# First attention: PSUM banks regrouped from three and three to four and two

## What is computed

```python
q = (hidden_states @ Wq.T).reshape(B, S, H, D)      # S = 1024, H = 32 heads, D = 8
k, v = ...                                          # likewise; rope on q and k
scores = jnp.einsum('bhid,bhjd->bhij', q, k) * scale
bias = jnp.where(in_band, learnable_bias[:, clip(diag)], 0.0)   # 0 <= i - j < 128
scores = jnp.where(causal, scores + bias, -jnp.inf)
m = jnp.maximum(jnp.max(scores, axis=-1), off)      # a row's maximum
p = jnp.exp(scores - m[..., None])
denom = jnp.sum(p, axis=-1) + jnp.exp(off - m)
out = jnp.einsum('bhij,bhjd->bhid', p, v) / denom[..., None]
```

## Time and profile before

| | us |
|---|---|
| median of 3 runs | 1211.83 (1206.76 to 1213.01) |
| the profiled execution | 1214.93 |
| its span, first to last instruction | 1212.6 |
| first look alone (opening stretch) | 165 to 191.5 |
| eight groups of second look | 191.6 to 493 |

### The profile page before, as it was taken

The page is one execution under the profiler, slowest core; times in us unless marked ns, Lnnn a source line. Parts: engine busy times, 40 slices in busy tenths (PEclk is TensorE's granted clock), DMA queues, the critical chain, the costliest instruction groups (busy, mean ns, idle before and its releaser), DMA issues.

```text
span 1212.6 us, 21037 instructions
## 1 busy us (share of the span) xinstructions
PE 1015.3 (84%) x7768; PEld 671.0 (55%) x7768; DVE 812.0 (67%) x1979; ACT 584.5 (48%) x1231; POOL 319.0 (26%) x212
## 2 busy tenths in 40 slices
PE   1798768999999998699787678898988988889697
PEld 1587612333333333478565556676666766667575
DVE  6745887787777771479778546666666666666654
ACT  1533224556656567254444235545445555454264
POOL 4010230000000000000033105555545464555344
PEclk9999857999999999899989699999999999999998
DMA  7010254312332100110121000000000000000001
GB/s 165 1 70 3 87 132 66 60 36 47 62 67 52 27 11 1 36 53 18 70 70 35 1 1 1 2 1 1 2 1 1 1 2 1 2 1 1 1 1 35
DMA packets 24038, 37.12 MB, mean 31 GB/s; under 512 B 2992, under 2 KB 21040, under 8 KB 22160
## 3 DMA queue, kind: packets, MB, share of 16 engines
q1 hardware_dynamic: 23936, 35.78, 12.8%
HBM read 31.31 MB, written 4.27 MB: 29 GB/s over the span
## 4 chain that ended last, share of the span: by engine, by line
PE 62%; DVE 22%; issue 8%; ACT 5%; DMA 1%; SPq 1%; POOL 1%; DVEq 0%; POOLq 0%; ACTq 0%
PE bank L923 18%; PE pair L1207 6%; PE bank L1251 6%; PE bank L1057 6%; PE bank L1086 5%; PE bank L1047 4%; PE bank L989 4%; DVE mx L1586 4%; PE bank L1239 3%; PE bank L1072 3%; ACT PT L825 2%; DVE PT L1619 2%; PE bank L953 2%; DVE bank L1462 2%; DVE hL L1386 1%
## 5 line engine op out<-in xcount | busy, mean ns | idle before, releaser
L705 POOL TENSOR_SCALAR P<-P,rec 128x1024 f32<-128x1024 f32 (+7 forms) x128 | 220.4, 1724 | 228.3 <-DVE rec L1611 228.3
L825 ACT ACTIVATE PT<-bank 128x512 f32<-128x512 f32 (+3 forms) x384 | 165.7, 493 | 103.7 <-PE bank L1072 87.7
L1462 DVE CUSTOM_DVE_ANT_0 bank<-bank,stripS 128x512 f32<-128x512 f32 (+3 forms) x256 | 148.9, 606 | 54.6 <-PE bank L1047 51.7
L1047 PE MATMUL bank<-KT,QT 96*128 96x512 bf16 (+3 forms) x384 | 126.5, 365 | 26.8 <-DVE MX L1462 11.9
L1239 PE MATMUL bank<-ident,P 128*128 128x128 f32 x576 | 99.0, 281 | 45.9 <-DVE PT L1619 33.7
L1057 PE MATMUL bank<-QT,KT 128*128 128x512 bf16 (+3 forms) x384 | 112.9, 336 | 12.9 <-ACT PT L825 11.0
L1207 PE MATMUL pair<-KH,QH 128*128 128x512 f16 (+3 forms) x576 | 115.4, 328 | 5.6 <-ACT P L872 4.2
L1251 PE MATMUL bank<-PT,VH 128*128 128x128 f16 x1728 | 117.2, 219 | 0.1
L872 ACT ACTIVATE P<-pair,nm 128x1024 f32<-128x1024 f32 (+7 forms) x128 | 95.6, 747 | 43.8 <-DVE nm L1590 43.8
L1251 PEld LDWEIGHTS bank<-PT,VH 128*128 128x128 f16 x1728 | 107.1, 98 | 2.8 <-DVE PT L1619 0.2
L1619 DVE TENSOR_TENSOR PT<-bank,PT 128x384 f16<-128x384 f32 (+1 forms) x192 | 99.7, 547 | 11.8 <-ACT PT L713 11.8
(11 more groups left out here) (178 smaller groups left out, 1920.0 us busy)
## 6 DMA issues: line engine op xcount, KB each, us to landing
stripS<-band_rows SPq DMA_DIRECT2D x32, 128.0 KB, 2.1
KT<-qk_dram SPq DMA_DIRECT2D x21, 192.0 KB
qk_dram<-parts SPq DMA_DIRECT2D x12, 256.0 KB, 2.4
cprow<-cp SPq DMA_DIRECT2D x9, 256.0 KB, 11.1
stripT<-seq_dram SPq DMA_DIRECT2D x24, 88.0 KB, 9.1
q_raw<-w_gu SPq DMA_DIRECT2D x4, 512.0 KB, 4.0
w_raw<-w_q SPq DMA_DIRECT2D x2, 1024.0 KB, 5.9
w_raw<-w_dense SPq DMA_DIRECT2D x2, 1024.0 KB, 5.4
```

The lines of the kernel that those rows point to most:

```text
L705: pool.tensor_scalar(rows, rows, rec1[:, m % 4:m % 4 + 1], None, ALU.mult).then_inc(s["pn"], 1)
L825: act.activation(PT[:, jb % 2, h, o:o + ni], bank[2 + i2 % 3][:, 0:ni], ACT.Exp).then_inc(s["s2_exp"], 1)
L1047: pe.matmul(ring_bank(use)[:, 0:nj], queries(g)[0:ROWS, h, P * ib:P * (ib + 1)], KT3[0:ROWS, g % 3, h, j0:j0 + nj], start=True, stop=True) ...
L1462: dve.tensor_tensor_reduce(out, out, stripS[:, h, HALF - nj:HALF], 1.0, LOWEST, ALU.add, ALU.max, mx).then_inc(s["s1_max"], 1)
```

## The change

Bank 5 moves from the ring to the second look. The ring has banks 0 and 1, and a use waits for the use two places earlier; second-look tiles rotate through banks 2 to 5, and product i waits for the exponential of tile i-4. No instruction is added, removed or moved on any engine; the banks of the tiles and the counts of the waits are what differs.

```diff
--- before.py
+++ after.py
@@ -409,14 +409,14 @@
                 RING += [("s", i, 0) for i in look1_at(g, st)] + ([turn(g, st)] if turn(g, st) else [])
         RING += [("o", NG - 1, 0), ("o", NG - 1, 1)]
         at_ring = {u: i for i, u in enumerate(RING)}
-        RING_BANKS = (0, 1, 5)
+        RING_BANKS = (0, 1)
 
         def ring_bank(use):
-            return bank[RING_BANKS[at_ring[use] % 3]]
+            return bank[RING_BANKS[at_ring[use] % 2]]
 
         def wait_ring(eng, use):
 
-            i = at_ring[use] - 3
+            i = at_ring[use] - 2
             if i >= 0:
                 kind, n, h = RING[i]
                 if kind == "s":
@@ -822,7 +822,7 @@
                                 if TB * g + jb >= 2:
                                     act.wait_ge(s["pv"], TB * g + jb - 1)
                                 o = i0 - jb * P
-                                act.activation(PT[:, jb % 2, h, o:o + ni], bank[2 + i2 % 3][:, 0:ni], ACT.Exp).then_inc(s["s2_exp"], 1)
+                                act.activation(PT[:, jb % 2, h, o:o + ni], bank[2 + i2 % 4][:, 0:ni], ACT.Exp).then_inc(s["s2_exp"], 1)
                         if st == 0 and g:
                             outputs(g - 1)
                         use = turn(g, st)
@@ -1052,9 +1052,9 @@
                 i2 = at_s2(g, jb, h, c)
                 if jb == 0 and h % 2 == 0 and c == 0:
                     pe.wait_ge(m_in[h // 2], 32 * (g + 1))
-                if i2 >= 3:
-                    pe.wait_ge(s["s2_exp"], i2 - 2)
-                ins = pe.matmul(bank[2 + i2 % 3][:, 0:ni], KT3[:, g % 3, h, P * jb:P * (jb + 1)], queries(g)[:, h, i0:i0 + ni],
+                if i2 >= 4:
+                    pe.wait_ge(s["s2_exp"], i2 - 3)
+                ins = pe.matmul(bank[2 + i2 % 4][:, 0:ni], KT3[:, g % 3, h, P * jb:P * (jb + 1)], queries(g)[:, h, i0:i0 + ni],
                                 start=True, stop=True)
                 if band_of(i0, ni, jb)[0] <= 0:
                     ins.then_inc(s["s2"], 1)
@@ -1069,7 +1069,7 @@
                     for q in range(4):
                         rows = slice(STRIP_ROWS * q, STRIP_ROWS * (q + 1))
                         first = STRIP_ROWS * (3 - q) + at
-                        ins = pe.matmul(bank[2 + at_s2(g, jb, h, c) % 3][rows, 0:n], flipb[:, :], stripT[:, g % 2, h, first:first + n],
+                        ins = pe.matmul(bank[2 + at_s2(g, jb, h, c) % 4][rows, 0:n], flipb[:, :], stripT[:, g % 2, h, first:first + n],
                                         start=False, stop=True, skip_group_check=True)
                     ins.then_inc(s["s2"], 1)
```

## The result

The changed kernel takes **1253.92 us** (median of 4 runs, 1252.86 to 1256.22) against 1212.42 us for the kernel before in the same comparison (4 runs, 1206.76 to 1216.19). The ratio is **1.0349**, 95% interval 1.0305 to 1.0392: slower by 41.5 us. Forecast were 1250 us and slower, with a range of 1224 to 1268.

What follows compares the result with a forecast made beforehand. DVE bounds the opening; in the groups PE, DVE and ACT form one chain, PE leading. Terms sum to +38.2 us on the profiled 1214.93, giving 1253.1; less 3.1 to the median, 1250 us, range 1224 to 1268.

Steps and rivals of the forecast that it cites:

- opening: First attention, 165 to 191.5 us, 60 first-look tiles, no second look: two banks hold back strip reduces, +9.6 us.
- part 2: Four second-look banks: product i waits for the exponential of i-4 instead of i-3; -1.5 us a group, -1.8 in the last.
- first group: First group of four heads after the opening, without output turns: 6.2 - 1.2 - 1.5 = +3.5 us.
- five usual groups: The five groups of four heads after the first: 6.2 - 1.5 = 4.7 us each, +23.5 us.
- group with 36 tiles: Seventh group, only 36 first-look tiles left: the stalls of steps 0 to 12 and slightly more gain, +3.4 us.
- Part 1: First-look ring from three banks to two: tile i waits for the reduce of i-2; +6.2 us a usual group, opening +9.6.
- the list of second-look waits: Usual group, PE's later waits for ACT: 0.31 (0.30 goes), 0.36, 0.48, 0.17 and 0.17 us; gain summed to -1.5 a group.
- steps 8 to 12: Usual group, where three first-look tiles meet only two of the second look: 2.3 us of the two-bank ring's loss.
- A: Rival: two banks are enough, DVE catches up, only removed ACT waits count after the opening; about -15 us, 1196; chance 0.08.
- B: Rival: stalls and gains cancel in the groups, only the opening and last group count, +9.6 and -1.8, 1220 us; chance 0.10.
- C: Rival: four second-look banks give nothing, as values products pin PE to ACT or it gets no lead; +50.5, 1262; chance 0.12.
- D: Rival: the clock swings, two falls in each of eight groups, 38 + 16 us and more, 1266 and up; chance 0.10.

Runs made afterwards that it cites:

- the kernel without part 2: Against the kernel before, the first look's ring cut from three banks to two, the second look keeping three, bank 5 idle: 1260.24 us, ratio 1.0362.
- forward schedule: Changed banks (two and four) with four first-look tiles in steps 0 to 3, three in 4 to 9, two or three after: 1231.37 us, 1.0143 against the kernel before.
- the even: Changed kernel with three first-look tiles in every step, instead of two in steps 0 and 1 and four in 14 and 15: 1236.45 us, 1.0191 against the kernel before.

## Why the prediction was right, point by point

The sign and the mechanism came out: the ring of two makes PE wait for DVE, in the opening and in every group, and the kernel without part 2 and the one with the opening's third bank back show it. The total is nearer than the terms deserve. The forecast left the clock out of its sum, and said so. The third column below is an estimate of what the banks did: steps that ran at the lower clock in one of the two kernels are replaced by the same step at full clock in another group, and the last group by its length in the run with two and four banks and the forward schedule (28.08 us against 29.77 before, both at 1.00).

| | forecast | banks, at like clock | clock | measured |
|---|---|---|---|---|
| opening | +9.6 | +8.7 | 0 | +8.7 |
| first group | +3.5 | +3.2 | -1.3 | +1.9 |
| five usual groups | +23.5 | +21.0 | +5.3 | +26.3 |
| group with 36 tiles | +3.4 | +2.3 | +1.0 | +3.3 |
| last group | -1.8 | -1.7 | +0.7 | -1.0 |
| together | +38.2 | +33.5 | +5.7 | +39.2 |

- **Opening.** The 17th tile's product began at 165.43, and the first group at 200.32, 34.9 us; before 165.38 and 191.58, 26.2. The sum had 8.5 for this and 1.1 for the small tiles ahead of it; these did take 2.0 us longer (10.0 from the first product to the last reduce, 8.0 before), but all of it hid in the DMA wait, since this execution also began them 0.9 us earlier.
- **First group.** Before, the clock fell in its steps 13 to 15, which took 8.2 us instead of 6.9; the changed kernel has no fall there.
- **Five usual groups.** They are 220.4 us against 194.1. At full clock a group is 42.55 against 38.34, 4.2 longer, where 4.7 was walked. Two of them, at a clock of 0.88, are 3.2 us longer together than at the others' pace, and the others, at 0.95 to 0.97, have 0.8 to 1.0 each of their own; before, only two of the five held a fall.
- **Together.** Measured are +39.2 to the end of the attention and +0.4 behind it; the profiled span grew by 39.6 us. The medians differ by 41.5; the interval of the ratio covers 39.6.

So the banks alone were put 4.7 us too high, and the clock, which was left out of the sum, brought 5.7: that these cancel is luck. The lower clock is not an accident of the one execution: the mean granted clock of the four runs of the changed kernel is 0.920 to 0.932, that of the kernel before in all comparisons 0.930 to 0.951.

Inside a usual group the terms were not all right either. Part 1 was put at 6.2 and measured, alone, at 5.1 with a fall of the clock on both sides (the group walked, 39.33 us, holds one). Part 2 was put at 1.5 and measured at 0.8. The step that failed there is the list of second-look waits: 0.30 and 0.36 of it (steps 5 and 6) stand directly ahead of a first-look tile that has to wait for its bank as well, and taking them away gave nothing; without them the list makes the 0.8 that was measured. I had raised the wait behind it (0.25 to 0.60) and so had the right net (1.3 less 0.66 is 0.6 in steps 5 to 7, and part 1 alone measured 0.6 there), but booked a gain on one side and a loss on the other, which made the case "part 2 gives nothing" look 12 us away; it is 6.6.

By place, at full clock: from step 13 on, 1.3 us were forecast and 1.6 came; before it 3.4 were forecast and 2.6 came. The mis-sized term is steps 8 to 12, put at 2.3 and measured at 1.5; the outputs turns (1.2) came at 1.3. Steps 0 and 1, put at +0.1, came at -0.3, all of it in step 0.

Of the rivals, A and B are out: the groups did not keep their 38 us. C is out by the trace, though only by half of the distance at which it was put; the two medians alone would not exclude it. D came in part, 5.7 us of the 39.2 where it was priced at 16 and more.

## What to carry to other kernels

A bank moved from one ring to another is priced by both rings' waits in program order, not by the idle share of the engines: here the ring that lost one was read by an engine idle a quarter of the time and still cost 5.1 us a group, against 0.8 gained. Where two waits follow each other on one engine, removing the first can give nothing, as the 0.31 and 0.36 us here did. Compare groups at the same granted clock before pricing anything: a fall of 3.4 us was worth 1.0 us, more than the bank gained. Before trading buffers, look at where the tiles stand: moving six first-look tiles to steps in which their reader was idle gave 9 us with the banks as they were (part of it clock), and banks that are idle in one phase can be lent to the ring of that phase.

## What the runs showed of the hardware

With two buffers between PE and DVE at the lower clock, a product of 512 columns and its strip reduce alternate at 1.46 us a pair, with plain reduces of 0.29, 0.42, 0.55 or 0.69 us hidden while the next product runs.

In the eight groups the clock was at its lower level for 14.1 us before and 45.0 us in the changed kernel, of which 3.8 and 4.1 are the end of the opening's low stretch. Each of the three falls before and the six after began in steps 13 to 15 of a group, or within 0.2 us of their end; there stand the maxima turn and, with two banks, PE's longest wait for DVE (1.1 us). Ahead of the fall at 279.48 PE was busy 2.11 of 3.48 us, at a granted clock of 1.00; in the stretch at the lower level that followed it was busy nearly all the time:

```profile
279.50:289.70 10.20, 9.63 (x67) 3.42 (x67) 6.45 (x19) 2.83 (x8) 0.16 (x1) 0.50 0.27 53
```

The same steps with the same waits also passed without a fall, from 321.78 to 330.21. With two banks and the even or forward schedule the fourth group stayed at 1.00, with PE's busy share of 88 to 89% hardly above the changed kernel's 87%. What decides for a fall was not settled.
